# A recurrent kernel whose engine programs keep their calls and change the order

## Chip, cores and metric

The kernel runs on one core of a Trainium2 chip. The metric is the device time of one execution in microseconds; three runs of the kernel before took 3046.1, 3058.06 and 3063.58 us, median 3058.06.

## What is computed

One layer on `x` of 4 x 512 tokens, width 256, float32. Cut to what matters:

```python
xn = layernorm(x)
mixed = silu(causal_conv4(xn @ W_qkv))          # 16 q heads, 16 k heads, 32 v heads of 128
q = l2norm(q) * 128 ** -0.5;  k = l2norm(k)     # each used by two v heads
beta = sigmoid(xn @ W_b);  g = -exp(A_log) * softplus(xn @ W_a + dt_bias)
# for each token t, state S (128 x 128 for each v head):
S = S * exp(g[t])
S = S + beta[t] * k[t][:, None] * (v[t] - k[t] @ S)[None, :]
o[t] = q[t] @ S
o = o * rsqrt(mean(o * o) + 1e-6) * norm_w * silu(xn @ W_z)
s = o @ W_out
out = x + s * silu(ffn(xn))                      # ffn: 8 experts, top 2, and a shared one
```

## The kernel before, in words

Three blocks run one after the other: `prepare_block` (layer norm, gates), `ffn_block`, and `recurrent_block`, which takes some 2500 of the 3060 us and is the only one touched. Every engine has its own program, written out by hand as a list of calls; an engine runs its calls in that order, and semaphores (`wait_ge`, `then_inc`) tie the engines to each other. So a call that waits also holds all calls behind it on its engine.

The recurrent block has 16 x 4 = 64 steps (`i` over the 16 key heads, `b` over the 4 sequences). A step takes one key head with its two value heads and 512 tokens, in 4 chunks of 128. It is pipelined over two steps: step n projects and prepares its own q, k, v and the triangular matrix of each chunk (`bmat`), while it finishes the inverse of the matrices of step n-1 and runs the scan of step n-1 over its chunks c = 0 to 3. `p` and `r` are the buffers of the two.

What the calls do, with lines of the profile:

- TensorE: `project(j)` (L807) is a 128 x 512 projection from `w_in`; j = 1 is k, 0 is q, 2 and 3 are the two v heads. `by_token(j)` (L824) transposes its result after convolution and silu (it waits for `mixed_done`). `join_w` (L752), `join_x` (L761 to 763), `halves_w` (L772), `halves_x` (L781) join the inverses of 32 x 32 blocks to one of 128; between `join_w` and `join_x` stands ScalarE's `take_join` (L1004), behind `join_x` VectorE's `join` (L1218), between `halves_w` and `halves_x` ScalarE's `take_halves` (L1011), behind `halves_x` VectorE's `halves` (L1223). `halves_w` also waits for six DMAs (`full_in`), which SP issues when VectorE's last `merge` has transposed `xq` (L1338). `solve(c)` (L694), `attend(c)` (L704, L711) and `read_state(c)` (L679, L682) are the scan; `solve(0)` waits for `x64_done`, which `halves` signals. `spread_rows` (L845), `merge_w` (L854), `merge_x` (L863) build the inverses of the 32 x 32 blocks of this step. `gated_transpose` (L723), `project_out` (L732) and `project_z` (L740) belong to the output.
- ScalarE: `first_tap` (L1048) starts the convolution, `silu(j)` (L1062) ends it, `squares_by_token` (L1075), `take_v` (L1085), `take_updates` (L962), `take_state_part` (L969), `exp_decay` (L1020), `take_merge` (L1094), `gate_z` (L997), `squares` (L981), `scale_out_weights` (L1026, in one step of four).
- VectorE: `taps(j)` (L1260, three instructions) the rest of the convolution, `gating(n, g)` (L1204, four instructions, all operands in SBUF) the product o x o_r x z of head g, `k_beta` (L1272 to 1279), `b_of_head` (L1288), `new_state`, `output`, `residual` the scan, `compact` (L1307), `decayed_k` (L1301), `substitute` (L1314 to 1330), `merge` (L1335, 1338), `scores_of_head` (L1294), `add_out` (L1210).
- GpSimd: `decays_by_beta(g)` (L1459), which waits for `k_beta`; `log_decays` (L1424, 1428, 1433); `blocks8` and `mask_level` (L1485), `rows8` (L1498), `q_norms` (L1473 to 1481), `k_norms` (L1466), `output_norms` (L1410 to 1416), whose result `o_r` the gating takes.
- SP issues the DMAs: the next step's rows, the diagonal blocks `bq` from `bmat`, and at the end of the step `invT` (L654) and `inv` (L656).

Of the kernel before, what the change touches and what calls it, by code (L numbers as in the profile page):

```python
# [22 lines left out]
BATCH, T, D = 4, 512, 256  # L23
# [451 lines left out]
def recurrent_block(nc, x, w_in_dram, w_z_dram, w_out_dram, norm_dram, keep, g_rows, out):  # L475
# [10 lines left out]
    with ExitStack() as ctx:  # L486
# [183 lines left out]
        def _(pe):  # L670
# [67 lines left out]
            def project_z(tb, c):  # L738
                for m in range(KT):
                    last = nc.tensor.matmul(ps[Z_BANK[c // 2]][:, (c % 2) * D:(c % 2 + 1) * D],  # L740
                                            xnT[:, m, tb * T + c * C:tb * T + (c + 1) * C], w_z[:, m, :],
                                            start=(m == 0), stop=(m == KT - 1))
                if c % 2:
                    last.then_inc(z_ps, 1)

            def join_w(n):

                pe.wait_ge(xqT_done, n(XT))
                pe.wait_ge(b_done, n(2))
                for u in range(U):  # L750
                    for k in (0, 2):
                        last = nc.tensor.matmul(ps[TRI][BLOCKS[k + 1], u * Q:(u + 1) * Q], bmat[BLOCKS[k], u, BLOCKS[k + 1]],  # L752
                                                xqT[BLOCKS[k], u, :], start=True, stop=True)
                last.then_inc(w32_ps, 1)
# [34 lines left out]
            for i in range(NK):  # L789
                for b in range(BATCH):  # L790
# [78 lines left out]

                    project(1)  # L870
                    join_w(n)
                    project(0)
                    join_x(n)
                    by_token(1)
                    halves_w(n)
                    project(2)
# [9 lines left out]
                    read_state(1)  # L886
                    by_token(0)
                    solve(1)
                    k_products(0)
                    attend(1)  # L890
                    pe.wait_ge(wz_in, (i + (1 if b == 0 else 2)) * 16)
# [1 line left out]
                    project_z(tb, 0)  # L893
                    read_state(2)
                    project_z(tb, 1)
                    spread_rows()
                    solve(2)
                    pe.wait_ge(ksq_done, n(1) + 1)
                    pe.wait_ge(kw_done, n(2) + 2)
                    project_out(n, 0, loads)  # L900
                    project_out(n, 1, loads)
                    pe.wait_ge(qsq_done, n(1) + 1)
                    project_out(n, 2, loads)
                    attend(2)
                    by_token(2)
                    merge_w(0)
                    read_state(3)
                    merge_x(0)
# [1 line left out]
                    pe.wait_ge(acc_done, n(2) + 1)  # L910
                    project_z(tb, 2)
                    attend(3)
                    project_out(n, 3, loads)
                    merge_w(1)
                    project_z(tb, 3)
                    merge_x(1)
                    by_token(3)
            n = counts(NK, 0)
            read_state, solve, attend = scan_parts(1, n)
            join_w(n)  # L920
# [32 lines left out]
        def _(act):  # L953
# [82 lines left out]
            for i in range(NK):  # L1036
                for b in range(BATCH):
                    p, r = b % 2, 1 - b % 2
                    n = counts(i, b)
                    take_updates, take_state_part, squares = scan_parts((b - 1) % BATCH, n)  # L1040

                    def first_tap(j):

                        act.wait_ge(proj_ps, n(4) + ORDER.index(j) + 1)
                        act.wait_ge(mixed_done, n(4))
                        act.wait_ge(ksq_done, n(1))
                        act.wait_ge(qsq_done, n(1))
                        nc.scalar.activation(conv[:, j, :], ps[PROJ_BANK[j]][:, :], ACT.Copy,  # L1048
                                             scale=w_in[:, KT * 4 * P + j * KC + KC - 1:KT * 4 * P + (j + 1) * KC]).then_inc(conv0_done, 1)

                    def silu(j):

                        act.wait_ge(tap_done, n(12) + 3 * ORDER.index(j) + 3)
                        if j < 2:

                            act.wait_ge(qs_ps, n(3))
                            dst = qkT[p][:, j, :]
                        else:

                            act.wait_ge(v_ps, n(2))  # L1060
                            dst = mixed[:, j - 2, :]
                        nc.scalar.activation(dst, conv[:, j, :], ACT.Silu).then_inc(mixed_done, 1)  # L1062

                    def squares_by_token(j):

                        if j:
                            act.wait_ge(k_ps, n(1) + 1)
                            act.wait_ge(beta_done, n(4))
                            act.wait_ge(k_pow, n(2))
                        else:  # L1070
                            act.wait_ge(q_ps, n(1) + 1)
                            act.wait_ge(q_pow, n(5))
                        sums, done = ((q_sq, qsq_done), (k_sq, ksq_done))[j]
                        for c in range(NC_):
                            last = nc.scalar.activation(conv[:, j, c * C:(c + 1) * C], ps[TOK_BANK[j]][:, c * C:(c + 1) * C], ACT.Square,  # L1075
                                                        accum_out=sums[:, c:c + 1])
                        last.then_inc(done, 1)

                    def take_v(j):

                        act.wait_ge(v_ps, n(2) + j + 1)
                        act.wait_ge(k_pow, n(2) + 2)
                        act.wait_ge(r_done, n(6))
                        for c in range(NC_):
                            last = nc.scalar.activation(v[p][:, j * NC_ + c, :], ps[TOK_BANK[2 + j]][:, c * C:(c + 1) * C], ACT.Copy,  # L1085
                                                        scale=k_norm[:, c:c + 1])
                        last.then_inc(v_done, 1)

                    def take_merge(lv):

                        act.wait_ge(wq_ps, n(NL) + lv + 1)
                        act.wait_ge(x32_ps, n(1) + 1)
                        act.wait_ge(xq_ps, n(NL) + lv)
                        nc.scalar.activation(wq[:, :, :], ps[TRI][:, 0:U * Q].rearrange("p (u t) -> p u t", u=U), ACT.Copy,  # L1094
                                             scale=-1.0).then_inc(wq_done, 1)

                    first_tap(1)
                    take_join(n)
                    first_tap(0)
                    silu(1)  # L1100
                    if b == 2:
                        act.wait_ge(out_ps, n(2))
                        scale_out_weights(i + 2)
                    squares_by_token(1)
                    take_halves(n)
                    silu(0)
                    first_tap(2)
                    take_updates(0)
                    take_transposes(n, 0)
                    first_tap(3)  # L1110
                    take_transposes(n, 1)
                    take_state_part(1)
                    take_updates(1)
                    silu(2)
                    exp_decay((b + 1) % BATCH, n(4) + 8, n(2) + 2, 0)
                    take_state_part(2)
                    squares_by_token(0)
                    squares(0)
                    take_updates(2)
                    exp_decay((b + 1) % BATCH, n(4) + 8, n(2) + 2, 1)  # L1120
                    silu(3)
                    take_merge(0)
                    squares(1)
                    take_state_part(3)
                    take_updates(3)
                    squares(2)
                    gate_z(n, 0)
                    squares(3)
                    take_merge(1)
                    take_v(0)  # L1130
                    gate_z(n, 1)
                    take_v(1)
            n = counts(NK, 0)
# [17 lines left out]
        def _(dve):  # L1151
# [93 lines left out]
            for i in range(NK):  # L1245
                for b in range(BATCH):
# [93 lines left out]
                    gating(n, 0)  # L1340
                    taps(1)
                    join(n, r)
                    taps(0)
                    k_beta()
                    gating(n, 1)
                    halves(n, r)
                    taps(2)
                    b_of_head(0)
# [5 lines left out]
                    new_state(1)  # L1354
                    output(1)
                    compact()
                    residual(2)
                    decayed_k(0)
                    decayed_k(1)
                    substitute()  # L1360
                    new_state(2)
                    output(2)
                    add_out(n, (b - 2) % BATCH, 0)
                    residual(3)
                    merge(0)
                    scores_of_head(0)
                    scores_of_head(1)
                    output(3)
                    add_out(n, (b - 2) % BATCH, 1)
                    merge(1)  # L1370
# [32 lines left out]
        def _(pool):  # L1403
# [38 lines left out]
            for i in range(NK):  # L1442
                for b in range(BATCH):
# [65 lines left out]
                    decays_by_beta(1)  # L1509
                    log_decays((b + 1) % BATCH, i * (16 * BATCH) + 16 * (b + 2), n(2) + 2, n(4) + 4)  # L1510
                    blocks8()
                    rows8()
                    mask_level(0)
                    q_norms()
                    k_norms()
                    mask_level(1)
                    output_norms(n, 1 - p)
            n = counts(NK, 0)
            output_norms(n, 1)

# [78 lines left out]
```

## Time and profile before

| | us |
|---|---|
| median of three runs | 3058.06 |
| profiled execution | 3062.27 |
| its span | 3060.6 |
| TensorE matmul busy | 2701.9 (88%) |
| TensorE weight load busy | 1974.6 (65%) |
| VectorE busy | 2185.7 (71%) |
| ScalarE busy | 1632.1 (53%) |
| GpSimd busy | 1093.0 (36%) |

The mean granted clock of TensorE is 0.966 of full speed. The recurrent loop begins at 513 us. Shares of busy time are averages over the blocks; for one step the timeline of each engine is read, with the idle time before an instruction and, in brackets, what ended it. "issue" in the brackets means that the profile names no releaser.

### The profile page before, as it was taken

The page shows a single profiled execution, that of the slowest core. Times are in us where ns is not written, and L with a number is a line of the kernel's source. Part 1 is how long each engine was busy: PE and PEld are TensorE (multiplying, and loading weights), DVE is VectorE, ACT ScalarE, POOL GpSimd, SP SyncE. Part 2 cuts the span into 40 slices and gives each one's busy share as a digit, 9 for nine tenths or more (in the row PEclk, how much of TensorE's full clock was granted, in tenths as well). Part 3 has the DMA queues.
Part 4 walks back from the last instruction along what each step waited for, and adds up shares of the span by engine and source line. Part 5 has one row for each costly group of instructions (what it writes and reads, how often), then busy time and mean ns, then how long its engine had stood idle before and what let it go on. Part 6 is the DMA issues. An engine that isn't in the chain of part 4 may idle for free.

```text
span 3060.6 us, 88021 instructions
## 1 busy us (share of the span) xinstructions
PE 2701.9 (88%) x34330; PEld 1974.6 (65%) x34330; DVE 2185.7 (71%) x4880; ACT 1632.1 (53%) x5068; POOL 1093.0 (36%) x1391
## 2 busy tenths in 40 slices
PE   3399997999999999999999999999999999999995
PEld 2155555667667766666666666676667667776664
DVE  3223324778887888888888888888888888888883
ACT  2111111666665666666666666666666666666662
POOL 0221012334444444444434444444444444444430
PEclk9799997999999999999999999999999999999997
DMA  1521121111111111111111111111111111111111
GB/s 40 154 59 39 20 58 46 42 47 44 38 46 37 47 45 47 45 45 46 46 46 46 46 46 46 46 46 46 46 46 46 46 46 46 46 46 46 46 46 58
DMA packets 225646, 146.87 MB, mean 48 GB/s; under 512 B 187456, under 2 KB 195936, under 8 KB 225120
## 3 DMA queue, kind: packets, MB, share of 16 engines
q1 hardware_dynamic: 219104, 123.58, 14.1%
q0 software_dynamic: 6144, 17.83, 2.6%
q8 instruction: 268, 4.39, 0.6%
q14 instruction: 130, 1.06, 0.1%
HBM read 115.81 MB, written 2.70 MB: 39 GB/s over the span
## 4 chain that ended last, share of the span: by engine, by line
PE 63%; issue 12%; POOL 4%; DVE 3%; ACT 1%; POOLq 0%; DVEq 0%; ACTq 0%
PE rps L807 13%; PE rps L732 7%; PE rps L740 6%; PE rps L694 4%; PE rps L824 3%; PE rps L711 3%; PE rps L679 3%; PE rps L837 3%; PE rps L863 3%; PE rps L854 3%; PE rps L704 3%; PE rps L682 2%; PE rps L772 2%; PE rps L781 2%; PE rps L723 2%
## 5 line engine op out<-in xcount | busy, mean ns | idle before, releaser
L1260 DVE SCALAR_TENSOR_TENSOR conv<-rps,w_in,conv 128x509 f32<-128x509 f32 (+2 forms) x768 | 571.4, 744 | 91.2 <-ACT conv L1048 73.1
L807 PE MATMUL rps<-xnT,w_in 128*128 128x512 f32 x1024 | 534.3, 647 | 13.5 <-DVE cols L1242 13.5
L1459 POOL TENSOR_TENSOR decay_b<-decay,beta_k 128x512 f32<-128x512 f32 x128 | 133.4, 1063 | 587.9 <-DVE beta_k L1276 587.9
L1204 DVE SCALAR_TENSOR_TENSOR gated<-o,o_r,z 128x128 f32<-128x128 f32 x528 | 339.9, 704 | 2.9 <-POOL o_r L1416 2.1
L962 ACT ACTIVATE upd<-rps 128x256 f32<-128x256 f32 x260 | 100.9, 388 | 381.4 <-PE rps L694 381.4
L1048 ACT ACTIVATE conv<-rps,w_in 128x512 f32<-128x512 f32 x256 | 175.9, 687 | 238.0 <-PE rps L807 235.3
L807 PEld LDWEIGHTS rps<-xnT,w_in 128*128 128x128 f32 x1024 | 184.7, 201 | 155.8 <-issue 134.6
L740 PE MATMUL rps<-w_z,xnT 128*128 128x256 f32 x1040 | 279.2, 391 | 1.0 <-ACT z L997 0.7
L732 PE MATMUL rps<-w_outn,gatedT 128*128 128x256 f32 x1056 | 252.8, 383 | 1.0 <-ACT gatedT L991 0.7
L441 DVE TENSOR_TENSOR silu_g<-fps_u,silu_g 128x512 f32<-128x512 f32 x68 | 47.0, 691 | 277.5 <-PE fps_u L460 128.3
L732 PEld LDWEIGHTS rps<-w_outn,gatedT 128*128 128x128 f32 x1056 | 192.4, 192 | 22.8 <-ACT gatedT L991 1.1
L740 PEld LDWEIGHTS rps<-w_z,xnT 128*128 128x128 f32 x1040 | 183.1, 191 | 22.2 <-ACT z L997 1.5
L411 POOL DMA_DIRECT2D scale<-comb_rows x96 | 64.2, 697 | 315.5 <-DVE hid L444 223.7
L1410 POOL TENSOR_TENSOR o_t<-o_sq,q_mean 128x8 f32<-128x8 f32 x65 | 13.1, 201 | 449.1 <-ACT gated L981 449.1
L981 ACT ACTIVATE gated<-o 128x128 f32<-128x128 f32 x520 | 156.7, 310 | 31.1 <-DVE o L1186 28.8
L1020 ACT ACTIVATE decay<-log_d,cols 128x128 f32<-128x128 f32 x520 | 167.0, 405 | 4.7 <-POOL log_d L1433 3.9
L1335 DVE TENSOR_TENSOR xq<-rps,xq 128x256 f32<-128x256 f32 x128 | 54.3, 424 | 160.7 <-PE rps L863 160.7
L460 PE MATMUL fps_g<-xnT,wg 128*128 x272 | 131.3, 606 | 41.0 <-DVE silu_g L441 28.7
L1165 DVE SCALAR_TENSOR_TENSOR resid<-rps,cols,v 128x128 f32<-128x128 f32 x390 | 118.7, 346 | 65.5 <-PE rps L679 63.7
L1433 POOL TENSOR_TENSOR log_d<-log_d,sums_row 128x512 f32<-128x512 f32 x130 | 162.6, 1271 | 5.4
L1085 ACT ACTIVATE v<-rps,k_norm 128x128 f32<-128x128 f32 x512 | 145.6, 371 | 28.3 <-PE rps L824 28.3
L711 PE MATMUL rps<-upd,scores 128*128 128x128 f32 x1040 | 159.6, 276 | 0.0
(216 smaller groups left out, 6389.4 us busy)
## 6 DMA issues: line engine op xcount, KB each, us to landing
sums_row<-g_rows SPq DMA_DIRECT2D x65, 1024.0 KB, 5.1
scale<-comb_rows POOLq DMA_DIRECT2D x40, 256.0 KB, 5.6
w_in<-in_w_in SPq DMA_DIRECT2D x17, 520.0 KB, 3.4
bq<-bmat SPq DMA_DIRECT2D x256, 32.0 KB, 2.0
inv<-xq SPq DMA_DIRECT2D x256, 32.0 KB, 1.9
w_z<-in_w_z SPq DMA_DIRECT2D x17, 256.0 KB, 2.6
w_out<-in_w_out SPq DMA_DIRECT2D x17, 256.0 KB, 5.2
invT<-xqT SPq DMA_DIRECT2D x128, 32.0 KB, 1.9
```

The lines of the kernel that those rows point to most:

```text
L711: last = nc.tensor.matmul(ps[OUT][:, g * P:(g + 1) * P], scores[r][:, g * NC_ + c, :], upd[:, g * P:(g + 1) * P], start=True, stop=True)
L732: last = nc.tensor.matmul(ps[OUT_BANK[c // 2]][:, (c % 2) * D:(c % 2 + 1) * D], gatedT[:, g, c * C:(c + 1) * C], w_outn[:, g, :], start=(g ...
L740: last = nc.tensor.matmul(ps[Z_BANK[c // 2]][:, (c % 2) * D:(c % 2 + 1) * D], xnT[:, m, tb * T + c * C:tb * T + (c + 1) * C], w_z[:, m, :] ...
L807: last = nc.tensor.matmul(ps[PROJ_BANK[j]][:, :], w_in[:, m * 4 * P + j * P:m * 4 * P + (j + 1) * P], xnT[:, m, b * T:(b + 1) * T], start= ...
L981: last = nc.scalar.activation(gated[:, c, g * P:(g + 1) * P], o[:, c, g * P:(g + 1) * P], ACT.Square, accum_out=o_sq[:, u:u + 1])
L1020: last = nc.scalar.activation(decay[:, u, :], log_d[:, u, :], ACT.Exp, bias=col(k, NLO, u))
L1048: nc.scalar.activation(conv[:, j, :], ps[PROJ_BANK[j]][:, :], ACT.Copy, scale=w_in[:, KT * 4 * P + j * KC + KC - 1:KT * 4 * P + (j + 1) * ...
L1085: last = nc.scalar.activation(v[p][:, j * NC_ + c, :], ps[TOK_BANK[2 + j]][:, c * C:(c + 1) * C], ACT.Copy, scale=k_norm[:, c:c + 1])
L1204: nc.vector.scalar_tensor_tensor(gated[:, c, part], o[:, c, part], o_r[:, u:u + 1], z[:, c, part], ALU.mult, ALU.mult).then_inc(gated_done, 1)
L1260: nc.vector.scalar_tensor_tensor(conv[:, j, shift:T], ps[PROJ_BANK[j]][:, 0:T - shift], w_in[:, k:k + 1], conv[:, j, shift:T], ALU.mult, A ...
L1433: nc.gpsimd.tensor_tensor(log_d[:, us, :], log_d[:, us, :], sums_row[:, 1, us, :], ALU.add).then_inc(g_done, 1)
L1459: nc.gpsimd.tensor_tensor(decay_b[:, us, :], decay[:, us, :], beta_k2[:, us].unsqueeze(2).to_broadcast([P, NC_, C]), ALU.mult).then_inc(db ...
```

## The change

The same calls in another order, on TensorE, ScalarE, VectorE and GpSimd; no call is added or removed, and no wait is changed inside a call.

```diff
@@ TensorE, the step
                     project(1)
                     join_w(n)
+                    join_x(n)
                     project(0)
-                    join_x(n)
                     by_token(1)
                     halves_w(n)
...
                     solve(1)
+                    by_token(2)
                     k_products(0)
                     attend(1)
...
                     project_z(tb, 1)
+                    solve(2)
                     spread_rows()
-                    solve(2)
...
                     project_out(n, 2, loads)
+                    project_out(n, 3, loads)
                     attend(2)
-                    by_token(2)
                     merge_w(0)
...
                     attend(3)
-                    project_out(n, 3, loads)
+                    by_token(3)
                     merge_w(1)
                     project_z(tb, 3)
                     merge_x(1)
-                    by_token(3)
@@ ScalarE, the step
                     first_tap(1)
                     take_join(n)
+                    silu(1)
                     first_tap(0)
-                    silu(1)
-                    if b == 2:
-                        act.wait_ge(out_ps, n(2))
-                        scale_out_weights(i + 2)
                     squares_by_token(1)
                     take_halves(n)
                     silu(0)
                     first_tap(2)
+                    if b == 2:
+                        act.wait_ge(out_ps, n(2))
+                        scale_out_weights(i + 2)
                     take_updates(0)
+                    first_tap(3)
                     take_transposes(n, 0)
-                    first_tap(3)
                     take_transposes(n, 1)
+                    silu(2)
                     take_state_part(1)
                     take_updates(1)
-                    silu(2)
                     exp_decay((b + 1) % BATCH, n(4) + 8, n(2) + 2, 0)
+                    squares_by_token(0)
+                    exp_decay((b + 1) % BATCH, n(4) + 8, n(2) + 2, 1)
                     take_state_part(2)
-                    squares_by_token(0)
                     squares(0)
                     take_updates(2)
-                    exp_decay((b + 1) % BATCH, n(4) + 8, n(2) + 2, 1)
                     silu(3)
+                    take_v(0)
                     take_merge(0)
...
                     squares(2)
-                    gate_z(n, 0)
                     squares(3)
                     take_merge(1)
-                    take_v(0)
+                    gate_z(n, 0)
                     gate_z(n, 1)
                     take_v(1)
@@ VectorE, the step
                     gating(n, 0)
                     taps(1)
                     join(n, r)
+                    gating(n, 1)
                     taps(0)
                     k_beta()
-                    gating(n, 1)
                     halves(n, r)
...
                     compact()
+                    decayed_k(0)
                     residual(2)
-                    decayed_k(0)
                     decayed_k(1)
                     substitute()
                     new_state(2)
                     output(2)
+                    scores_of_head(0)
+                    residual(3)
                     add_out(n, (b - 2) % BATCH, 0)
-                    residual(3)
+                    scores_of_head(1)
                     merge(0)
-                    scores_of_head(0)
-                    scores_of_head(1)
                     output(3)
@@ GpSimd, the step
                     blocks8()
+                    mask_level(0)
                     rows8()
-                    mask_level(0)
+                    mask_level(1)
+                    k_norms()
+                    output_norms(n, 1 - p)
                     q_norms()
-                    k_norms()
-                    mask_level(1)
-                    output_norms(n, 1 - p)
```

## Rows read from the trace of the kernel before

**Rows 1.** Page, part 1, and line L807 by source (ns min/median/max, first to last start).

```profile
PE 2701.9 (88%) x34330; PEld 1974.6 (65%) x34330; DVE 2185.7 (71%) x4880; ACT 1632.1 (53%) x5068; POOL 1093.0 (36%) x1391
...
L807 PE MATMUL rps<-xnT,w_in x1024: 592/592/1222, 513.0 to 2971.6; 128*128 128x512 f32 x171
```

**Rows 2.** Waits of TensorE, 516 to 2957 us: us in total, times, longest.

```profile
PE rps L694 <- issue: 118.4, 59, 2.5
PE rps L824 <- ACT qkT L1062: 43.0, 63, 1.7
PE rps L863 <- issue: 12.4, 13, 1.2
...
PE rps L772 <- issue: 6.6, 4, 1.9
```

**Rows 3.** Timeline of TensorE, one step: start, us, instructions, [idle before <- releaser].

```profile
1492.29 1.88 PE L807 MATMUL rps<-xnT,w_in 128*128 128x512 f32 x4
...
1498.65 1.11 PE L772 MATMUL rps<-invT,bmat 64*64 64x64 f32 x16
...
1501.60 1.14 PE L781 MATMUL rps<-inv,wh 64*64 64x64 f32 x16
...
1506.60 0.68 PE L694 MATMUL rps<-v,inv 128*128 128x128 f32 x4 [2.38 <-issue]
1507.12 1.88 PE L807 MATMUL rps<-xnT,w_in 128*128 128x512 f32 x4
...
1530.06 1.88 PE L807 MATMUL rps<-xnT,w_in 128*128 128x512 f32 x4
```

**Rows 4.** Timeline of VectorE in the same step.

```profile
1492.74 1.09 DVE L1204 SCALAR_TENSOR_TENSOR gated<-o,o_r,z 128x128 f32<-128x128 f32 x4
1494.93 2.31 DVE L1260 SCALAR_TENSOR_TENSOR conv<-rps,w_in,conv 128x509 f32<-128x509 f32 x3 [1.10 <-ACT conv L1048]
...
1501.64 4.26 DVE L1204 SCALAR_TENSOR_TENSOR gated<-o,o_r,z 128x128 f32<-128x128 f32 x4
1505.83 0.67 DVE L1223 COPY inv<-rps 64x512 f32<-64x512 f32 x1
1506.43 2.30 DVE L1260 SCALAR_TENSOR_TENSOR conv<-rps,w_in,conv 128x509 f32<-128x509 f32 x3
...
1518.19 0.21 DVE L1321 TENSOR_TENSOR x<-x,t 128x48 f32<-128x48 f32 x1
```

**Rows 5.** Timeline of GpSimd in the same step.

```profile
1501.50 2.08 POOL L1459 TENSOR_TENSOR decay_b<-decay,beta_k 128x512 f32<-128x512 f32 x2 [9.14 <-DVE beta_k L1276]
1503.55 1.94 POOL L1424 TENSOR_TENSOR log_d<-sums_row,cols 128x1024 f32<-128x1024 f32 x1
...
1518.03 1.02 POOL L1475 TENSOR_TENSOR q_rinv<-q_t,mhalf 128x4 f32<-128x4 f32 x1
```

**Rows 6.** Timelines of another step: TensorE, VectorE, GpSimd.

```profile
1005.05 0.68 PE L694 MATMUL rps<-v,inv 128*128 128x128 f32 x4 [0.76 <-issue]
...
1001.73 2.63 DVE L1204 SCALAR_TENSOR_TENSOR gated<-o,o_r,z 128x128 f32<-128x128 f32 x4
...
1005.84 1.90 POOL L1424 TENSOR_TENSOR log_d<-sums_row,cols 128x1024 f32<-128x1024 f32 x1 [2.16 <-DMA sums_row<-g_rows]
```

**Rows 7.** Timeline of ScalarE in the step of rows 3.

```profile
1494.84 0.38 ACT L1004 ACTIVATE wq<-rps 128x256 f32<-128x256 f32 x1
...
1497.33 0.62 ACT L1062 ACTIVATE qkT<-conv 128x512 f32<-128x512 f32 x1
```

**Rows 8.** Timeline of SP's queue in the same step.

```profile
1492.84 1.78 SPq L654 DMA_DIRECT2D invT<-xqT  x2
1494.66 2.58 SPq L656 DMA_DIRECT2D inv<-xq  x4
```

**Rows 9.** Busy time and granted clock (PEclk) of the loop; TensorE behind another wait.

```profile
513.00:2971.00 2458.00, 2256.08 (x32529) 1697.30 (x32530) 1999.72 (x4499) 1526.50 (x4832) 1010.04 (x1270) 0.98 0.16 45
...
1584.27 3.45 PE L807 MATMUL rps<-xnT,w_in 128*128 128x512 f32 x4
```

## The prediction

> **What bounds the kernel now.** I read the page first: TensorE is busy 88% of the span, VectorE 71%, ScalarE 53%, GpSimd 36% [rows 1]. TensorE sets the time, so only what it waits for can be won; a call that moves on another engine counts when TensorE waits for its result. Nothing outside the 64 steps of the recurrent loop changes. The first projection matmul starts at 513.0 us and the last at 2971.6 us [rows 1]; it is the fourth of `project(3)`, which in the step of rows 3 began 14.8 us after `project(1)` and put its fourth matmul 1.4 us behind its first. So 63 steps take 2971.6 - 16.2 - 513.0 = 2442.4 us, 38.77 us each. An undisturbed step is 1530.06 - 1492.29 = 37.77 us [rows 3]. I call T the start of a step's `project(1)`.
>
> The waits of TensorE in the loop, grouped by line, come next, then the timelines of all engines over one step [rows 2 to 8]. Two of them are in every step: `solve(0)` (L694), 118.4 us in total, and `by_token(1)` (L824), 43.0 us. The others (L863, 12.4 us, and L772, 6.6 us in four steps, are the largest) come in some steps only.
>
> The wait of `solve(0)`. It starts 1506.60, after 2.38 us of idleness [rows 3]. The profile names no releaser, so I followed its semaphores in the code: it needs `x64_done`, VectorE's `halves` (L1223). That ran from 1505.83 to 1506.50 although its input, `halves_x` on TensorE (L781), was there at 1502.7; before it stands `gating(n, 1)`, four instructions that took 4.26 us [rows 3, 4]. The same four instructions for head 0 took 1.09 us at 1492.74 [rows 4]. What differs is GpSimd: it is idle at 1492.74, and at 1501.50 it runs `decays_by_beta` (2.08 us) and then the first `log_d` add (1.94 us), which end at 1505.49 [rows 5]; the gating ends 1505.90. A second step shows it from the other side: at 1001.73 the same gating took 2.63 us, because GpSimd stood still for 2.16 us after its first 2.08 us, waiting for a DMA; there `solve(0)` waited 0.76 us and not 2.38 [rows 6]: 1.63 us less gating, 1.62 us less waiting. So VectorE's gating stops while GpSimd works on large tiles, and all of it reaches TensorE.
>
> The Trainium skill ("SBUF — State Buffer", the sections on the engine ports) has the mechanism: a VectorE instruction with two SBUF tensor inputs shares a read port with GpSimd, as an exclusive lock for the whole instruction. The trace agrees: 4.26 against 1.09 us.
>
> **The change, part by part.**
>
> (1) `gating(n, 1)` goes from behind `k_beta()` to ahead of `taps(0)`. GpSimd can't be in `decays_by_beta` then, since that waits for `k_beta`, which now comes later. Cost 1.09 us in place of 4.26: VectorE is 3.17 us ahead at `halves`. From T, the new order of VectorE: `taps(1)` ends about T+4.95, as now; `join` 1.25 to 6.2; gating 1.09 to 7.35; `taps(0)` 2.25 to 9.6; `k_beta` 0.8 to 10.4. `halves` then waits for its input and not for VectorE. The wait of 2.38 us at `solve(0)` goes. What is late next: `decay_b` on GpSimd starts at T+10.2 and not T+9.2, ends T+12.3, and `b_of_head` wants it at T+13.8: covered. The `log_d` adds behind it end at T+18.1; the expensive VectorE work beside them (taps, `bmat`, residual) has one input in PSUM, and the taps took 2.31 us at 1494.93 without GpSimd and 2.30 at 1506.43 beside it [rows 4, 5].
>
> (2) `join_x(n)` ahead of `project(0)` on TensorE, `silu(1)` ahead of `first_tap(0)` on ScalarE. `by_token(1)` waits for `silu(1)`, which starts at 1497.33, when `taps(1)` (end 1497.24) and `first_tap(0)` (end 1497.44) are done [rows 4, 7]. So `silu(1)` can start only 0.09 us sooner, T+4.95. But `project(0)` then ends at T+5.6 instead of `join_x` at T+5.05, because `join_x` needs ScalarE's `wq`, done at 1495.22 = T+2.93 [rows 7], while `join_w` is through at T+2.5: a new wait of 0.45 us at `join_x`. The 0.67 us at `by_token(1)` becomes 0.45 at `join_x` plus some 0.05: gain 0.15 us.
>
> (3) `by_token(3)` from the end of the step to behind `attend(3)`. The work is the same 0.49 us, but it no longer stands between `merge_x(1)` and `project(1)`. All that follows from `merge_x(1)` by VectorE and SP is therefore 0.49 us later against T: `merge(1)`'s transpose ends at T+1.02 and not T+0.53. Behind it SP issues six small DMAs, 1492.84 to 1497.24 [rows 8], which `halves_w` (L772) needs. Over the 63 steps I took the last issue's end plus 1.41 us (the least that L772 ever started behind it) as the time of landing: 5.28 to 6.61 us after the transpose, and in four steps L772 came only at 7.3 to 7.7 (the four waits of L772 for "issue", [rows 2]). TensorE is at `halves_w` 5.8 us after the transpose now, and at (T+5.63+0.58) - (T+1.02) = 5.2 in the new order. Over those 63 values the mean wait is 0.67 us. Before, this wait was largely swallowed by the one at `solve(0)`; now it is on the path: a loss. `halves_w` thus starts at T+6.89 on average.
>
> (4) The rest. From `halves_w` (1498.65) to the next `project(1)` (1530.06) are 31.41 us [rows 3]; without the 2.38 and 0.19 us of smaller stops, the sum of TensorE's own starts from call to call is 28.84 us. Then I walked the four engines through the new order to see which wait shows. `solve(0)` needs `x64_done` at T+11.6, TensorE is there at T+12.2. `by_token(2)`, now behind `solve(1)`, needs `silu(2)`, T+17.2 against T+17.85. `solve(2)` (ahead of `spread_rows`) needs `residual(2)`, T+22.6 against 22.8, the tightest. `spread_rows` needs GpSimd's `b_rows` at T+22.4 against 23.3. `merge_w(0)` needs `substitute` by T+27.95 against 28.4. `merge_x(0)` needs ScalarE's `take_merge(0)`, 29.55 against 30.15, with `take_v(0)` ahead of it from 26.75. Each is covered, by 0.2 to 0.9 us, so I cost them at nothing; if the tightest cover is gone, 0.2 to 0.5 us in a step. The moves inside ScalarE (`scale_out_weights`, `squares_by_token(0)`, `gate_z(0)`) and `add_out`, `scores_of_head`, `decayed_k` on VectorE exchange places within idle time.
>
> (5) Sporadic waits. A wait for `b_rows` (L845), there in some steps now, goes with the cover of 0.9 us; that of L863 (12.4 us), for which no engine is named, I keep [rows 2].
>
> (6) The clock. In the loop the granted clock is 0.98 on average [rows 9]. It falls from 2.4 to 1.2 GHz right behind some of the long waits: the four matmuls of `project(3)` took 3.45 us at 1584.27, behind a wait of 2.37, and 1.88 at 1507.12 [rows 3, 9], 1.57 us more. I find 23 such dips in the loop, 36 us. In the step of rows 6, with 0.76 us of waiting, `project(3)` follows at the full clock. With waits of 0.45 and 0.67 us I expect nearly all dips gone and leave 5 us.
>
> The Trainium skill ("TensorE: Matmul & The Clock Gate", "HAM oscillation") has the clock fall only when TensorE is left waiting for long; by it the short gaps that remain would bring no dip at all, and the sum would be 5 us less.
>
> **The sum.** New step: 6.89 + 28.84 = 35.73 us. 64 steps: 2286.7; plus 5.6 us for the first step's surplus as now, 12.4 for L863, 5 for the clock: 2309.7. Now: 2442.4 + 37.8 = 2480.2. Gain 170.5 us. The profiled execution took 3062.3 us (span 3060.6), so 2891.8; the median of the runs is 4.2 us lower. I forecast 2889.
>
> **Rivals.**
>
> A. The port is met in a new place. `q_norms` moves behind `output_norms`, beside `gating(n, 0)`, and contains 1.02 us of pow. If that holds the gating, VectorE is late for `taps(1)` by up to 1.02 + 1.02 + 1.09 - 2.64 = 0.5 us: 32 us over 64 steps, 2921. Against it: the subtraction with two SBUF inputs at 1518.19 took 0.21 us in the middle of just that pow [rows 4, 5].
>
> The Trainium skill ("SBUF — State Buffer", the engine ports) makes no difference by tile size, so by it that subtraction would be blocked as well, and A would come; the time would be the 2921.
>
> B. One of the thin covers in (4) fails in every step, 0.5 to 1.3 us: 32 to 83 us, 2920 to 2970. For it: they are 0.2 us thin, and DMA landings vary by 1.3 us.
>
> C. Nothing won: `solve(0)`'s wait is only moved, because ScalarE or the DMA behind `halves_w` takes its place in full. It would need 2.7 us more in each step than I find: 3058.
>
> D. Slower: the clock. TensorE has three short waits where it had two, and the clock stays at 1.2 GHz for a longer stretch in every step. A stretch of some 10 us at half clock costs up to 5 us of a step; from 2.7 us per step on (a stretch of 5.4 us each) the kernel is slower, and with 3.5 us it is 2889 + 64 x 3.5 = 3113. Against it: the step of rows 6.
>
> **How the numbers follow.** Forecast 0.66, A 0.08, B 0.18, C 0.04, D 0.04. Half a per cent is about what a measurement can tell. Faster 0.93, same 0.03, slower 0.04. Low end: the DMA wait falls to 0.3 us and the clock never dips, 64 x 0.37 + 5 = 29 us less, 2860. High end: B with 0.9 us in each step, 2947.
>
> **What would show it.** The four gatings (L1204) all 1.1 us; no wait at L694; new waits of 0.45 us at L761 behind `wq` and about 0.7 us at L772; L824 near zero; granted clock 1.00; a step of 35.7 us. Wrong if L694 still waits for `x64_done`, if L845, L854 or a second L694 wait in every step, or if the clock keeps its dips.

## The result

The changed kernel takes 2894.96 us (median of four runs, 2888.94 to 2897.01), the kernel before 3059.86 (four runs): ratio 0.947, 95% interval 0.944 to 0.950. The forecast was 2889, in a range of 2860 to 2947. In the profiled executions the loop of 64 steps, taken from the start of the first `join_w` to that of the 65th, went from 2477.7 to 2306.5 us; the prediction had 2480.2 and 2309.7.

The page of the changed kernel, parts 1 and 2, answers to rows 1: TensorE runs the same instructions in a span that is 173.3 us shorter; 67.2 us of that are less busy time and 106.1 us less idle time. VectorE's busy time is 184 us less, also with the same instructions.

```profile
span 2887.3 us, 88021 instructions
PE 2634.7 (91%) x34330; PEld 1955.5 (68%) x34330; DVE 2002.1 (69%) x4880; ACT 1620.9 (56%) x5068; POOL 1073.0 (37%) x1391
...
PEclk9799999899999999999999999999999999999997
```

The waits of TensorE in the loop, 516 to 2820 us (us in total, times, longest), to be held against rows 2:

```profile
PE rps L761 <- ACT wq L1004: 35.1, 64, 4.6
PE rps L772 <- DVE inv L1218: 30.9, 51, 0.9
PE rps L863 <- issue: 17.5, 28, 1.4
PE rps L694 <- DVE resid L1165: 4.0, 9, 0.8
PE rps L772 <- issue: 2.1, 2, 1.1
PE rps L694 <- issue: 1.2, 3, 0.7
```

The wait at `solve(0)` (L694), 118.4 us before, is gone; L824 (43.0) isn't in the list any more; in their place stand `join_x` (L761), 0.48 us in each step but one of 4.6, and `halves_w` (L772), 33.0 us together.

One step of the changed kernel on TensorE, VectorE and GpSimd (start, us, instructions, [idle before <- releaser]), to be held against rows 3 to 5:

```profile
1285.96 0.21 PE L761 MATMUL rps<-wq,xq 32*32 32x32 f32 x1 [0.48 <-ACT wq L1004]
...
1286.59 1.98 PE L807 MATMUL rps<-xnT,w_in 128*128 128x512 f32 x4
1288.65 0.66 PE L824 MATMUL rps<-cst,qkT 128*128 128x128 f32 x4
1289.64 1.11 PE L772 MATMUL rps<-invT,bmat 64*64 64x64 f32 x16 [0.34 <-DVE inv L1218]
...
1294.16 1.06 PE L837 MATMUL rps<-qkT 128*128 128x128 f32 x8
1295.05 0.61 PE L694 MATMUL rps<-v,inv 128*128 128x128 f32 x4
```

```profile
1283.86 1.14 DVE L1204 SCALAR_TENSOR_TENSOR gated<-o,o_r,z 128x128 f32<-128x128 f32 x4
...
1289.20 1.12 DVE L1204 SCALAR_TENSOR_TENSOR gated<-o,o_r,z 128x128 f32<-128x128 f32 x4
1290.25 2.30 DVE L1260 SCALAR_TENSOR_TENSOR conv<-rps,w_in,conv 128x509 f32<-128x509 f32 x3
...
1293.77 0.68 DVE L1223 COPY inv<-rps 64x512 f32<-64x512 f32 x1 [0.54 <-PE rps L781]
```

```profile
1284.06 1.01 POOL L1475 TENSOR_TENSOR q_rinv<-q_t,mhalf 128x4 f32<-128x4 f32 x1
...
1293.12 2.04 POOL L1459 TENSOR_TENSOR decay_b<-decay,beta_k 128x512 f32<-128x512 f32 x2 [7.33 <-DVE beta_k L1276]
```

Both gatings take 1.1 us. `halves` (L1223) now waits for its input, 0.54 us, and not for VectorE, and `solve(0)` follows `k_products(1)` (L837) without a stop. `decays_by_beta` starts 2.8 us behind the end of the gating of head 1.

### The profile page after: what moved, and what is told of

Same layout as the page of the kernel before. It is cut to its first block, busy times and chain, and to the rows that moved or that the text cites. A ratio compares the mean times of both kernels' runs of the same rounds, so it can differ in the third digit from the quotient of the medians.

```text
span 2887.3 us, 88021 instructions
## 1 busy us (share of the span) xinstructions
PE 2634.7 (91%) x34330; PEld 1955.5 (68%) x34330; DVE 2002.1 (69%) x4880; ACT 1620.9 (56%) x5068; POOL 1073.0 (37%) x1391
## 4 chain that ended last, share of the span: by engine, by line
PE 67%; DVE 7%; ACT 3%; issue 3%; DMA 1%; SPq 1%; POOL 0%; DVEq 0%; POOLq 0%; ACTq 0%
PE rps L807 12%; PE rps L732 8%; PE rps L740 8%; DVE conv L1260 5%; PE rps L694 4%; PE rps L824 4%; PE rps L711 4%; PE rps L837 3%; PE rps L863 3%; PE rps L679 3%; PE rps L854 3%; PE rps L704 3%; PE rps L682 3%; PE rps L772 3%; PE rps L781 2%
## 5 line engine op out<-in xcount | busy, mean ns | idle before, releaser
L807 PE MATMUL rps<-xnT,w_in 128*128 128x512 f32 x1024 | 506.0, 617 | 13.5 <-DVE cols L1242 13.5
L807 PEld LDWEIGHTS rps<-xnT,w_in 128*128 128x128 f32 x1024 | 175.2, 191 | 147.6 <-issue 124.1
L1410 POOL TENSOR_TENSOR o_t<-o_sq,q_mean 128x8 f32<-128x8 f32 x65 | 13.2, 204 | 687.6 <-ACT gated L981 687.6
L732 PE MATMUL rps<-w_outn,gatedT 128*128 128x256 f32 x1056 | 241.2, 381 | 1.1 <-ACT gatedT L991 0.7
L732 PEld LDWEIGHTS rps<-w_outn,gatedT 128*128 128x128 f32 x1056 | 201.5, 191 | 49.6 <-issue 23.8
L1062 ACT ACTIVATE qkT<-conv 128x512 f32<-128x512 f32 x128 | 80.6, 630 | 194.0 <-DVE conv L1260 194.0
L422 ACT ACTIVATE silu_g<-fps_g 128x512 f32<-128x512 f32 x68 | 40.6, 597 | 208.3 <-PE fps_g L460 208.3
L1204 DVE SCALAR_TENSOR_TENSOR gated<-o,o_r,z 128x128 f32<-128x128 f32 x528 | 150.4, 342 | 2.2 <-POOL o_r L1416 2.1
```

The costliest lines, as they stand in the source:

```text
L732: last = nc.tensor.matmul(ps[OUT_BANK[c // 2]][:, (c % 2) * D:(c % 2 + 1) * D], gatedT[:, g, c * C:(c + 1) * C], w_outn[:, g, :], start=(g ...
L807: last = nc.tensor.matmul(ps[PROJ_BANK[j]][:, :], w_in[:, m * 4 * P + j * P:m * 4 * P + (j + 1) * P], xnT[:, m, b * T:(b + 1) * T], start= ...
L1204: nc.vector.scalar_tensor_tensor(gated[:, c, part], o[:, c, part], o_r[:, u:u + 1], z[:, c, part], ALU.mult, ALU.mult).then_inc(gated_done, 1)
```

## The experiments

The theory: the gain is the gating freed from GpSimd, with the dips of the clock that hung on the wait at `solve(0)`; the rest of the reordering moves waits about. The rival: the order as a whole makes the room. All times are medians of four runs (ten for the second run), with the kernel before beside them on the same chip (3057.8 to 3059.4). Counts of clock falls are those of the granted clock's record in the profiled execution: a fall is a stretch at 1.2 GHz that begins between 560 and 2800 us of the span, which holds 59 to 64 of the steps, depending on the kernel.

**One move alone.**

```diff
@@ kernel before, VectorE
                     join(n, r)
+                    gating(n, 1)
                     taps(0)
                     k_beta()
-                    gating(n, 1)
```

> The kernel before with one call moved: gating(n, 1) ahead of taps(0) on VectorE; everything else in the old order. Theory (the port shared with GpSimd is the whole gain, the other moves bring nothing or less): the four gatings take 1.1 us, the wait of TensorE at solve(0) goes from 2.4 to under 0.3 us, the step from 37.8 to 35.4 us, the clock dips go, and the time is 2870 to 2890 us, no longer than that of the full change, because by_token(3) still stands between merge_x(1) and project(1) and hides half a microsecond of the DMA landing before halves_w. Rival (the other moves were needed to make room for it): without them b_rows, substitute or residual is late, TensorE waits at L845, L854 or L694 by 0.5 us or more per step, and the time is 2925 us or more.

Measured: 2902.89 us, ratio 0.950 (0.947 to 0.952). So 155 us of the whole change's 165 come with this one call. The rival's 2925 isn't reached. But the expected 2870 to 2890 are missed too: the time is 8 us over the changed kernel's, where I had expected it no longer. Waits between 560 and 2800 us:

```profile
PE rps L824 <- ACT qkT L1062: 41.3, 62, 0.7
PE rps L863 <- issue: 20.0, 24, 1.3
PE rps L772 <- DVE inv L1218: 8.8, 23, 0.7
PE rps L845 <- POOL b_rows L1498: 7.7, 12, 1.1
PE rps L772 <- issue: 5.0, 3, 1.9
```

The list shows what was expected, 0.67 us at L824, little at L772. What I hadn't expected is the clock: its record has 11 falls to 1.2 GHz in this stretch, 41 us long together. The changed kernel has one of 3.4 us there, the kernel before 21, 85 us. Of those 21, 13 stand at the wait of `solve(0)`, 2.1 to 2.5 us long; the other 8 stand at a wait of `halves_w` that follows the 0.67 us at `by_token(1)` closely.

**Everything but this move.**

```diff
@@ changed kernel, VectorE
-                    gating(n, 1)
                     taps(0)
                     k_beta()
+                    gating(n, 1)
```

> The changed kernel with one call put back: gating(n, 1) behind k_beta() again. Theory: the gatings beside GpSimd take 4.3 us again, solve(0) waits some 2 us, the step is 37.6 us, the clock dips come back in a part of the steps, and the time is 3020 to 3060 us. Rival (the gain comes from the new order as a whole, with slack for VectorE): solve(0) waits under 1 us and the time stays under 2975 us.

Measured: 3050.19 us (ratio 0.9996, 0.997 to 1.002): no difference to the kernel before that can be told. As expected, the gating beside GpSimd takes 4.26 us again, and `solve(0)` waits (last line: 560 to 2800 us); the clock falls 11 times, ten of them at that wait:

```profile
1350.56 4.26 DVE L1204 SCALAR_TENSOR_TENSOR gated<-o,o_r,z 128x128 f32<-128x128 f32 x4
1354.74 0.67 DVE L1223 COPY inv<-rps 64x512 f32<-64x512 f32 x1
...
PE rps L694 <- issue: 100.4, 57, 2.5
```

**What stops the gating.** The same order as before, the same place beside GpSimd; only the third operand of the gating of head 1 comes from PSUM (it isn't `z`, so the output isn't the layer's).

```diff
@@ kernel before, VectorE
-            def gating(n, g):
+            def gating(n, g, held=None):
...
-    gated[:, c, part], o[:, c, part], o_r[:, u:u + 1], z[:, c, part],
+    gated[:, c, part], o[:, c, part], o_r[:, u:u + 1],
+    z[:, c, part] if held is None else held[:, c * C:(c + 1) * C],
...
                     k_beta()
-                    gating(n, 1)
+                    gating(n, 1, ps[TOK_BANK[1]])
```

> The kernel before with its order unchanged; only the gating of head 1 reads its third operand from a PSUM bank (the k of by_token(1)) and not z from SBUF, so the product of that head isn't the reference's. The four instructions stand where they stood, beside GpSimd's decays_by_beta and log_decays. Theory (what stops them is the second SBUF input): they take some 1.2 us in all and not 4.26, the wait at solve(0) is under 0.5 us, and the time is that of the kernel with only the gating moved, 2895 to 2915 us. Rival (GpSimd's large tiles slow any VectorE instruction on SBUF, or the place behind k_beta is what costs): the gatings still take over 3 us and the time stays above 3030 us.

Measured: 2897.49 us, ratio 0.946 (0.941 to 0.952). By line (ns min/median/max), head 0 with `z` (and the gatings outside the steps) and head 1 with PSUM; then one step, GpSimd and VectorE:

```profile
L1204 DVE SCALAR_TENSOR_TENSOR gated<-o,o_r,z x272: 307/346/1982, 513.3 to 2883.6; 128x128 f32<-128x128 f32 x136
L1204 DVE SCALAR_TENSOR_TENSOR gated<-o,o_r,rps x256: 339/343/349, 529.1 to 2818.3; 128x128 f32<-128x128 f32 x128
...
1373.42 2.04 POOL L1459 TENSOR_TENSOR decay_b<-decay,beta_k 128x512 f32<-128x512 f32 x2 [9.17 <-DVE beta_k L1276]
...
1373.55 1.12 DVE L1204 SCALAR_TENSOR_TENSOR gated<-o,o_r,rps 128x128 f32<-128x128 f32 x4
```

All 256 took 339 to 349 ns, in all 64 steps while GpSimd was in `decays_by_beta`; in the same place four of them took 4.26 us with `z` from SBUF [rows 4]. Order and place are unchanged, so it is the second SBUF input, and the time is that of the moved gating. The wait at `solve(0)` is nearly gone (1.8 us in two places). What the Trainium skill ("SBUF — State Buffer", "Who interferes with whom") says, that a VectorE instruction with one SBUF input doesn't contend with GpSimd and one with two does, is thereby measured here. The clock falls 19 times in this run, 72 us together, though none of its waits is as long as the 2.4 us of before.

**`join_x` back behind `project(0)`.**

```diff
@@ changed kernel, TensorE
                     join_w(n)
-                    join_x(n)
                     project(0)
+                    join_x(n)
```

> The changed kernel with join_x(n) behind project(0) again on TensorE; silu(1) stays ahead on ScalarE. Theory (the 0.48 us at join_x only take the place of the wait at by_token(1), because both orders end at silu(1)): no wait at L761, one of 0.5 to 0.6 us at L824, the wait at L772 as it is, the time within 5 us of the changed kernel's 2895. Rival (the move of join_x is worth something by itself): the time is 2905 us or more.

Measured: 2967.52 us (2962.54 to 2973.74), ratio 0.970 (0.967 to 0.973): 72 us slower than the changed kernel. The theory (within 5 us) is wrong and the rival (2905 or more) holds. First the waits (560 to 2800 us), then one step, then the clock of that step (columns: stretch, length, busy time and instructions of PE, PEld, DVE, ACT, POOL, granted clock, DMA share, GB/s):

```profile
PE rps L824 <- ACT qkT L1062: 38.1, 61, 0.6
PE rps L772 <- DVE inv L1218: 24.8, 42, 1.1
PE rps L863 <- issue: 21.3, 31, 1.4
PE rps L772 <- issue: 14.6, 10, 1.8
...
1379.67 0.66 PE L824 MATMUL rps<-cst,qkT 128*128 128x128 f32 x4 [0.63 <-ACT qkT L1062]
1381.43 1.93 PE L772 MATMUL rps<-invT,bmat 64*64 64x64 f32 x16 [1.10 <-DVE inv L1218]
1383.29 3.78 PE L807 MATMUL rps<-xnT,w_in 128*128 128x512 f32 x4
...
1380.00:1384.00 4.00, 2.90 (x20) 2.36 (x19) 3.86 (x11) 1.93 (x10) 0.00 (x0) 0.65 0.63 167
1384.00:1388.00 4.00, 4.00 (x13) 1.68 (x12) 0.37 (x3) 1.32 (x2) 3.68 (x3) 0.50 0.30 121
1388.00:1392.00 4.00, 4.00 (x30) 3.05 (x29) 3.30 (x5) 0.38 (x1) 3.69 (x4) 1.00 0.00 0
```

The large waits sum to 99 us, against 81 in the same stretch of the changed kernel (L761, L772, L863). That is at most 18 us. The rest is the clock: 30 falls, 143 us at 1.2 GHz in place of 3.4, and half of 140 is 70. The pages agree: the two profiled executions are 80 us apart (2967.5 and 2887.3), and 68 of them are TensorE's busy time (2702.7 against 2634.7) for the same instructions. The four matmuls of `project(2)` take 3.78 us at 1383.29.

What the falls have in common I read from the traces of both kernels, step by step. Here the waits at L824 and at L772 stand only a `by_token(1)` of 0.7 us apart; 47 steps have both (over 0.2 us), and in 28 of them the clock falls. The other two of the 30 falls stand behind the 0.62 us at L824 alone. In the changed kernel 50 steps have two waits too (L761 and L772), but `join_x`, `project(0)` and `by_token(1)`, 3.3 us of work, stand between them: one fall. How long the two waits are doesn't explain it: here falls come behind pairs that sum to 0.97 us or more, and there 38 pairs with as much bring none. The first wait is 0.62 us here and 0.48 there; no run has the one length at the other distance.

The test of that: the same order with the second of the two waits taken away. The six DMAs behind `merge(1)` get two semaphores, so `halves_w` waits for `invT`, which it reads, and `halves_x` for `inv`.

```diff
@@ SP (a new semaphore inv_in)
-    sp.dma_start(inv[p][rows, :, rows], xq[rows, :, :]).then_inc(full_in, 16)
+    sp.dma_start(inv[p][rows, :, rows], xq[rows, :, :]).then_inc(inv_in, 16)
@@ TensorE, halves_w
-                pe.wait_ge(full_in, n(96))
+                pe.wait_ge(full_in, n(32))
@@ TensorE, halves_x
+                pe.wait_ge(inv_in, n(64))
                 pe.wait_ge(w64_done, n(1) + 1)
```

> The changed kernel with join_x(n) behind project(0) again, and the semaphores split. Without the split this order was 72 us slower than the changed kernel, with 30 falls of the granted clock in the loop (143 us at half) against 3 (24 us), though its waits are hardly longer: 0.62 us at L824 and, right behind, up to 1.8 us at L772. Theory (the clock falls because these two waits stand close together): without the one at L772 the falls go, under 8 are left, and the time is 2855 to 2880 us. Rival (the single wait of 0.62 at L824, or the order of join_x and project(0) itself, brings the falls): 15 or more are left and the time is above 2900 us.

Measured: 2853.05 us, 114 us less than without the split and 2 below the expected range. No fall stands in the steps at all (the only one between 560 and 2800 us, at 2789.7, comes behind the last of them), though `by_token(1)` (here L827) still waits 39.3 us in 63 places. So the rival, that the order or the single wait of 0.62 us brings the falls, is out. The expectation holds the 30 falls without the split, counted from 560 to 2800 us, against 3 (24 us) of the changed kernel, which go on behind its last step; in one and the same stretch it is 30 against 1. The mean clock of that stretch, without and with the split:

```profile
560.00:2800.00 2240.00, 2137.09 (x30945) 1626.37 (x30944) 1721.98 (x4272) 1430.53 (x4588) 932.01 (x1201) 0.97 0.17 47
...
560.00:2800.00 2240.00, 2173.89 (x32482) 1675.83 (x32481) 1806.07 (x4481) 1498.76 (x4807) 978.48 (x1260) 1.00 0.18 50
```

A single wait isn't always harmless, though. With 0.67 us at `by_token(1)`, the length of the old order, a fall came behind that wait with no other close to it in one place of the run with one move, in seven of the run with PSUM and in all four falls of the run with gating and split (below).

**The split alone, on the changed kernel.**

> The changed kernel with the six DMAs behind merge(1) counted on two semaphores: halves_w waits only for the two that fill invT, which it reads, and halves_x for the four that fill inv. Theory (the wait at L772 is the landing of the last of the six): it goes to nearly zero, the step to 35.3 us, the time by 30 to 40 us to 2855 to 2868 us. Rival (the wait at L772 is something else, such as VectorE's join): the time stays within 10 us of 2895.

Measured: 2845.66 us (2844.61 to 2850.4), ratio 0.931 (0.926 to 0.936) to the kernel before and 49 us under the changed one: the fastest of all. `halves_w` (here L774) has one wait left:

```profile
PE rps L763 <- ACT wq L1007: 30.9, 64, 0.5
PE rps L866 <- issue: 15.8, 23, 1.3
PE rps L696 <- DVE resid L1168: 3.8, 11, 0.8
...
PE rps L774 <- DVE invT L1221: 0.7, 1, 0.7
```

So the wait at L772 was the landing of DMAs that its reader didn't read. The gain is more than the 33 us of that wait. Between the two profiled executions it is 42.9 us (2887.3 to 2844.4): 36 less at L772, 4.0 of them behind the last step, and 5 less of TensorE's busy time. The other 6 of the 49 come from the changed kernel's profiled run being 6 us under its median. The expected 2855 to 2868 was too high by 9 us or more.

**`by_token(3)` back at the end of the step**, once without and once with the split.

```diff
@@ changed kernel, TensorE
                     attend(3)
-                    by_token(3)
...
                     merge_x(1)
+                    by_token(3)
```

> The changed kernel with by_token(3) put back to the end of TensorE's step, behind merge_x(1). Theory (the wait at halves_w is the landing of six DMAs issued behind merge(1), and by_token(3) at the end hides 0.49 us of it): the wait at L772 falls from 0.57 to 0.2 us in the mean, the step from 35.9 to 35.5 us, the time by 15 to 30 us to 2865 to 2880 us. Rival (the place of by_token(3) doesn't matter, or take_v(1) on ScalarE and with it project(0) comes late): the time is that of the changed kernel, 2890 to 2905 us, or more.

> The same split of the semaphores with by_token(3) back at the end of the step. With no wait left at L772, theory: the place of by_token(3) makes no difference, the time is within 6 us of the kernel with the split alone. Rival (by_token(3) behind merge_x(1) is worth something by itself, as the 7 us that it brought without the split could be): 8 us or more below it.

Measured: 2888.28 us without the split, 2853.79 with it: 7 us under the changed kernel, where 15 to 30 were expected, and 8 us over the one with the split alone. Without the split L772 does fall, from 33.0 to 16.6 us (560 to 2800), but L863 rises, and half of what was expected is lost:

```profile
PE rps L761 <- ACT wq L1004: 30.5, 63, 0.5
PE rps L863 <- issue: 29.1, 36, 1.4
PE rps L772 <- DVE inv L1218: 16.6, 34, 1.0
PE rps L694 <- DVE resid L1165: 6.1, 13, 0.8
```

With the split, nothing is won at L772, and L863 (21.2 against 15.8) and a wait at the last transposes (3.3) remain. Theory and rival of that run both miss: one had the place free of cost, the other a gain. Why L863, for which the profile names no releaser, depends on the order stays open.

**Gating and split in the old order, and three moves without the rest.**

```diff
@@ second of the two: kernel before, besides the gating; TensorE, then ScalarE
+                    join_x(n)
                     project(0)
-                    join_x(n)
...
                     project_out(n, 3, loads)
+                    by_token(3)
                     merge_w(1)
...
                     merge_x(1)
-                    by_token(3)
...
+                    silu(1)
                     first_tap(0)
-                    silu(1)
```

> The kernel before with two edits: gating(n, 1) ahead of taps(0), and the six DMAs behind merge(1) counted on two semaphores so that halves_w waits for two of them; all else in the old order. Theory: the wait at L772 is gone (it was 17.6 us in the kernel with only the gating moved), the clock falls in under 5 places instead of 12, and the time is 2865 to 2880 us; what is left against the changed kernel with the split, 2846 us, is the waits for b_rows (L845, 8 us) and 0.67 instead of 0.48 us in each step (12 us). Rival (the other moves are needed once the DMA wait is gone): over 2885 us.

> The kernel before with only three of the moves: gating(n, 1) ahead of taps(0) on VectorE; join_x ahead of project(0) on TensorE with silu(1) ahead of first_tap(0) on ScalarE; by_token(3) ahead of merge_w(1), behind project_out(3), on TensorE. All other calls in the old order. Theory (the remaining moves make room that nobody needs but for b_rows): L845 waits 8 us, the old order of scores_of_head on VectorE makes by_token(3) wait up to 0.5 us per step, the clock falls in under 5 places, the time is 2900 to 2930 us. Rival (the remaining moves are worth nothing): within 5 us of the changed kernel's 2895.

Measured: 2861.81 us and 2896.11 us. The first is 3 us under the expected range and 16 us over the fastest, with 13.2 us at `b_rows` (8 expected) and 42.0 at L827 (L824 before) where the fastest has 30.9 at `join_x`. Its clock falls four times, each time behind the single wait at L827, with no wait at `halves_w` (L774); one of the four, with `project(2)` (L810) at 3.59 us behind it:

```profile
1058.44 0.66 PE L827 MATMUL rps<-cst,qkT 128*128 128x128 f32 x4 [0.67 <-ACT qkT L1065]
1059.03 1.14 PE L774 MATMUL rps<-invT,bmat 64*64 64x64 f32 x16
1060.10 3.59 PE L810 MATMUL rps<-xnT,w_in 128*128 128x512 f32 x4
```

The second is the changed kernel's time within 1.2 us, 4 us under the theory's 2900, so here the rival holds: the fifteen or so other moves on four engines bring nothing that can be measured. They do take the waits for `b_rows`, 4.6 us in this run.

## Why the prediction was right, and where it wasn't

(1) The gating: right in mechanism and size. L694 lost 113 us, the gating is 1.1 us, and the two runs with one operand or one call changed show it from both sides. Rival A isn't what happens: the gating of head 0 at 1283.86 took 1.14 us beside the pow of `q_norms`, and 1.10 to 1.14 in all 63 steps where the two meet, against 1.09 in the kernel before. By the lock that the prediction takes from the Trainium skill ("SBUF — State Buffer"), held for the whole instruction at any tile size, rival A would have come; the measurement decides against it.

(2) The new wait at `join_x`: 0.48 us, forecast 0.45. But the step "gain 0.15 us" mis-sized what the order is worth, because it counted waits and not their effect on the clock. As a sum of waits it is right to some 0.3 us a step; in time the order is worth 72 us where `halves_w` waits too, and about 7 to the other side (2853 against 2846) where it doesn't.

(3) The loss at `halves_w`: mechanism right, shown by the split. The size was 0.67 us a step, measured 0.52. The four late landings of the kernel before were put into the mean, and the changed one had two. Worked again from the trace of before, the mean comes to 0.59 with the four and 0.49 without.

(4) The walk through the four engines found no cover gone in every step, and there was none: L694 behind `residual` waits in nine places, 4.0 us, the one that was named the tightest. Rival B stayed away.

(5) L845 went, as said. L863 was to stay at 12.4 us and is 17.5.

(6) The clock. "Nearly all dips gone" came true, with 3.4 us at half clock where 85 were; that gives some 41 us back (half of the difference, an estimate) against the 31 that the prediction took from 36 and 5. The reason given was wrong in part. The argument was the length of each wait; but already in the kernel before four of the 21 falls stand behind 0.67 us and then only 0.26 to 0.79. The kernel with only the gating moved has 0.67 us at `by_token(1)`, mostly less at `halves_w`, and 11 falls; with `join_x` back it is 30. What counts is also how close the waits stand. So the forecast was lucky here: the order that it took for worth 0.15 us a step is what keeps the clock up. Rival D was nearer than its 0.04 looks: one call in another place, and its mechanism costs 72 us, though that doesn't reach 170. The Trainium skill ("TensorE: Matmul & The Clock Gate", "HAM oscillation"), with the fall behind long waits, isn't enough to see this: no wait beside the 30 falls was over 1.8 us, and some falls stand behind 0.67 us alone. Where the two differ, the measurement decides.

For the loop the sum was 3 us too large (2309.7 against 2306.5). Of its terms the DMA wait was too large by 10 us and the 5 us left for the clock by 3; L863 was too small by 5, `join_x` by 2, and the 5 us at L694 were priced at nothing. These errors nearly cancel, which is luck. The forecast of 2889 lies 6 us under the median, while the 2891.8 for a profiled execution lies 3 us over the 2888.9 measured. The step between the two took 4.2 us off because the profiled run of before was that much over its median (2891.8 less 4.2 is 2887.6 and not 2889); the changed kernel's was 6 us under its own.

## What to carry to other kernels

When an instruction takes several times its own minimum, look at what the neighbour engine does in that moment, and move it to where that engine can't be working, because the engine waits for something that comes later; or give it an operand from PSUM. Two short waits of TensorE were cheaper here with 3.3 us of work between them than with 0.7, because of the clock. And a semaphore that counts a whole group of DMAs makes its waiter late by those that it doesn't read: one more semaphore was worth 49 us here.

## What the runs showed of the hardware that was not expected

The granted clock fell to 1.2 GHz in 28 of 47 steps with two waits, 0.62 us and then 0.25 to 1.8, and 0.7 us of work between them; in one of 50 steps with 3.3 us of work between two waits; and in no step of the order with the close waits once the second of them was taken away. A single wait of 0.67 us was followed by a fall in some places, four in the run with gating and split. GpSimd's small pow (128 x 4, 1.0 us) doesn't hold VectorE's instructions with two SBUF inputs (1.14 against 1.09 us for four), while its 128 x 512 and 128 x 1024 additions and products do (4.26 us). Whether the size or the operation makes the difference isn't tested.
